# Sliding-window attention scores as three products of split operands instead of one full-precision product

## What is computed

```python
q = split_heads(hidden_states @ wq)      # 16 heads of 128
k = split_heads(hidden_states @ wk)
v = split_heads(hidden_states @ wv)
q = _apply_rotary(q, cos, sin)
k = _apply_rotary(k, cos, sin)
valid = (k_pos > q_pos - WINDOW) & (k_pos <= q_pos)      # WINDOW is 256, Ln is 256
attn = jnp.einsum('bhqd,bhkd->bhqk', q, k) * scale
attn = jnp.where(valid, attn, neg)
attn = jax.nn.softmax(attn, axis=-1)
out = jnp.einsum('bhqk,bhkd->bhqd', attn, v)
return out @ wo
```

## Time and profile before

| | |
|---|---|
| time, median of 3 runs | 2634.21 us (2633.89 to 2636.63) |
| the profiled execution | 2631.4 us, of which the span of its instructions is 2629.7 us |
| self-attention (units 0 to 31) | about 36 to 1890 us of the span |
| context attention | about 1890 to 2280 us |
| experts | the rest |
| PE busy | 2512.0 us, 96% of the span |
| DVE, ACT, POOL busy | 1875.7, 958.9, 861.5 us |

### The profile page before, as it was taken

The page is one execution under the profiler, slowest core; times in us unless marked ns, Lnnn a source line. Parts: engine busy times, 40 slices in busy tenths (PEclk is TensorE's granted clock), DMA queues, the critical chain, the costliest instruction groups (busy, mean ns, idle before and its releaser), DMA issues. The chain is left out here.

```text
span 2629.7 us, 36626 instructions
## 1 busy us (share of the span) xinstructions
PE 2512.0 (96%) x12424; PEld 1885.8 (72%) x12424; DVE 1875.7 (71%) x3978; ACT 958.9 (36%) x2434; POOL 861.5 (33%) x696
## 2 busy tenths in 40 slices
PE   6999999999999999999999999999889999998894
PEld 5788888888888888888888888888634444442673
DVE  5887887666667666666766677777768878885657
ACT  2323223322222232222233222223257777776220
POOL 3211112321111232111123211122258888887000
PEclk8999999999999999999999999999989999999897
DMA  3222233221222222122222212222356676661003
GB/s 120 65 81 94 102 120 125 90 81 65 84 100 73 86 91 81 65 91 96 71 88 89 81 64 81 99 78 89 117 177 218 221 226 221 215 213 60 21 1 128
DMA packets 170150, 280.56 MB, mean 107 GB/s; under 512 B 15088, under 2 KB 81648, under 8 KB 169968
## 3 DMA queue, kind: packets, MB, share of 16 engines
q1 hardware_dynamic: 169968, 278.23, 31.4%
HBM read 185.37 MB, written 92.27 MB: 106 GB/s over the span
## 5 line engine op out<-in xcount | busy, mean ns | idle before, releaser
L539 PE MATMUL pj<-xnt,whi 128*128 128x512 f32 x2048 | 718.9, 412 | 7.3 <-DVE xnt L926 7.3
L705 ACT ACTIVATE pr<-sc,nmx 128x128 f32<-128x128 f32 (+1 forms) x512 | 210.6, 416 | 1011.2 <-DVE nmx L871 1008.1
L433 POOL TENSOR_TENSOR qt<-rot,swp 128x512 f32<-128x512 f32 x128 | 165.8, 1296 | 1038.0 <-DVE swp L847 1035.3
L539 PEld LDWEIGHTS pj<-xnt,whi 128*128 128x128 f32 x2048 | 388.1, 189 | 87.7 <-DVE xnt L926 8.1
L539 PE MATMUL pj<-xnt,wlo 128*128 128x512 f32 x1024 | 400.7, 391 | 0.0
L536 PE MATMUL pj<-whi,xnt 128*128 128x512 f32 x1024 | 358.5, 411 | 4.1 <-issue 4.1
L459 POOL TENSOR_TENSOR xprt<-xprt,xprt 128x512 f32<-128x512 f32 x256 | 320.6, 1284 | 83.6 <-PE ob L626 83.6
L762 ACT ACTIVATE xprt<-pj 128x512 f32<-128x512 f32 x512 | 290.8, 595 | 145.5 <-PE pj L615 143.9
L845 DVE TENSOR_TENSOR rot<-pj,trig 128x512 f32<-128x512 f32 x256 | 176.4, 689 | 137.2 <-PE pj L539 136.4
L955 DVE TENSOR_REDUCE xnmx<-sc 128x1 f32<-128x512 f32 x342 | 227.2, 680 | 65.0 <-PE sc L604 64.7
L433 POOL TENSOR_TENSOR kt<-rot,swp 128x512 f32<-128x512 f32 x128 | 164.8, 1287 | 304.4 <-DVE swp L847 304.4
(11 more groups left out here) (180 smaller groups left out, 4272.5 us busy)
## 6 DMA issues: line engine op xcount, KB each, us to landing
xnt<-xt_scratch SPq DMA_DIRECT2D x48, 1024.0 KB, 7.1
x_scratch<-xio SPq DMA_DIRECT2D x64, 512.0 KB, 3.6
xio<-x_scratch SPq DMA_DIRECT2D x48, 512.0 KB, 3.9
qst<-sq_scratch SPq DMA_DIRECT2D x192, 128.0 KB, 2.5
kst<-sk_scratch SPq DMA_DIRECT2D x192, 128.0 KB, 2.6
raw<-in_w_all_dram SPq DMA_DIRECT2D x64, 256.0 KB, 4.8
xt_scratch<-xnt SPq DMA_DIRECT2D x16, 1024.0 KB, 8.4
sq_scratch<-qp SPq DMA_DIRECT2D x32, 512.0 KB, 3.4
```

The lines of the kernel that those rows point to most:

```text
L433: nc.gpsimd.tensor_tensor(qk["QK".index(kind)][h][:, :, :].rearrange("p b n -> p (b n)"), rot[r % 2][:, :], swp[r % 2][:, :], ALU.add).the ...
L539: last = nc.tensor.matmul(bank[:, :], wpart[:, w, i * HD:(i + 1) * HD], moving, start=(k == 0), stop=(k == 3 * CB - 1))
L705: nc.scalar.activation(pr[:, a % 4, lo:hi], SC[a % 2][:, lo:hi], ACT.Exp, bias=nmx[:, a % 4, t:t + 1], accum_out=rsum[:, a % 4, t:t + 1]). ...
```

## The change

The turned queries and keys are no longer kept in float32. GpSimd adds in place into `rot`; ScalarE then rounds the sum into `qhi`/`khi` (`turn_round`, new), and GpSimd subtracts to get the rest `qlo`/`klo` (`turn_rest`, new). The scores wait for the rest, and each of the two score tiles is three float32r matmuls. `rope_mul` may reuse a `rot` buffer only after the rest is taken.

The rest parts need 16 KB, which come from the second set of Q weight chunks (and the wlo places beside it). So there is one set; the next group's Q chunks can only be converted after the last Q block of the old group (slot 8), and the weight schedule moves: V in slots 4 to 7, Q and K in slots 9 to 12. The load of the projections' input moves from slot 10 to 14, and the preparation of the context attention in the last unit moves some slots later, with its buffers at other places. The core of the diff:

```diff
-        qk = [[at_x2(f"{n}t{h}", [P, 2, L], F32, 40 + 8 * k + 2 * h) for h in range(HG)] for k, n in enumerate("qk")]
+        qkhi = [[at_x2(f"{n}hi{h}", [P, 2, L], F32R, 40 + 8 * k + 2 * h) for h in range(HG)] for k, n in enumerate("qk")]
+        qklo = [[at(f"{n}lo{h}", [P, 2, L], F32R, 60.5 + 2 * NCH + 40 * k + 2 * h) for h in range(HG)] for k, n in enumerate("qk")]
...
-            return NCH * g + 4 * ("QVKO" if g else "QKVO").index(kind) + c
+            return NCH * g + 4 * ("VQKO" if g else "QKVO").index(kind) + c
...
+        QK_PARTS = [(kind, c) for kind in "QK" for c in range(CB)]
+        QK_AT = ((0, 1, 2), (3, 4), (5, 6), (7,))
...
             if f % PAIRS == PAIRS - 1 and 0 < g < G:
-                if k < 4:
-                    return [(g, "Q", k)]
-                if k < 8:
+                if 4 <= k < 8:
                     return [(g, "V", k - 4)]
-                if k in (10, 11):
-                    return [(g, "K", 2 * (k - 10) + i) for i in range(2)]
+                if 9 <= k < 13:
+                    return [(g, *QK_PARTS[i]) for i in QK_AT[k - 9]]
...
-                if k == 10 and PAIRS <= u + 2 < UNITS:
+                if k == 14 and PAIRS <= u + 2 < UNITS:
                     sp.wait_ge(s_blk, number["K", u, 3] + 1)
                     load_xn(u + 2)
...
             def turn_add(kind, u, h):
                 r = place[kind, u, h]
                 pool.wait_ge(s_mul, r + 1)
-                if u:
-                    pool.wait_ge(s_sc, 8 * (u - 1) + 2 * h + 2)
-                nc.gpsimd.tensor_tensor(qk["QK".index(kind)][h][:, :, :].rearrange("p b n -> p (b n)"), rot[r % 2][:, :],
-                                        swp[r % 2][:, :], ALU.add).then_inc(s_rot, 1)
+                nc.gpsimd.tensor_tensor(rot[r % 2][:, :], rot[r % 2][:, :], swp[r % 2][:, :], ALU.add).then_inc(s_rot, 1)
+
+            def turn_rest(kind, u, h):
+                r, k = place[kind, u, h], "QK".index(kind)
+                pool.wait_ge(s_qkhi, r + 1)
+                nc.gpsimd.tensor_tensor(qklo[k][h][:, :, :].rearrange("p b n -> p (b n)"), rot[r % 2][:, :],
+                                        qkhi[k][h][:, :, :].rearrange("p b n -> p (b n)").bitcast(F32),
+                                        ALU.subtract).then_inc(s_qklo, 1)
...
             for s in range(-3, LAST + 1):
+                if s - 2 in at and at[s - 2][0] in "QK":
+                    turn_rest(*at[s - 2])
                 if s - 1 in at and at[s - 1][0] in "QK":
                     turn_add(*at[s - 1])
...
             def scores(a):
                 u, h, b = a // 8, a % 8 // 2, a % 2
-                pe.wait_ge(s_rot, place["K", u, h] + 1)
+                pe.wait_ge(s_qklo, place["K", u, h] + 1)
                 if a >= 2:
                     pe.wait_ge(s_exp, 2 * a - 2)
-                bank, qT, kT = SC[a % 2], qk[0][h][:, b, :], qk[1][h][:, b, :]
-                nc.tensor.matmul(bank[:, 0:P], qT[:, 0:P], kT[:, 0:P], start=True, stop=True)
-                nc.tensor.matmul(bank[:, P:3 * P], qT[:, P:2 * P], kT[:, 0:2 * P], start=True,
-                                 stop=True).then_inc(s_sc, 1)
+                bank, (qhi, khi), (qlo, klo) = SC[a % 2], (part[h][:, b, :] for part in qkhi), (part[h][:, b, :] for part in qklo)
+                for t in range(TB):
+                    out, rows, cols = bank[:, t * P:(2 * t + 1) * P], slice(t * P, (t + 1) * P), slice(0, (t + 1) * P)
+                    for k, (q, x) in enumerate(((qhi, khi), (qhi, klo), (qlo, khi))):
+                        last = nc.tensor.matmul(out, q[:, rows], x[:, cols], start=(k == 0), stop=(k == 2))
+                last.then_inc(s_sc, 1)
...
+            def turn_round(kind, u, h):
+                r = place[kind, u, h]
+                act.wait_ge(s_rot, r + 1)
+                if u:
+                    act.wait_ge(s_sc, 8 * (u - 1) + 2 * h + 2)
+                nc.scalar.activation(qkhi["QK".index(kind)][h][:, :, :].rearrange("p b n -> p (b n)"), rot[r % 2][:, :],
+                                     ACT.Copy).then_inc(s_qkhi, 1)
...
                 if s - 1 in at and at[s - 1][0] == "V":
                     v_evac(*at[s - 1][1:])
+                if s - 2 in at and at[s - 2][0] in "QK":
+                    turn_round(*at[s - 2])
...
                 if r >= 2:
-                    dve.wait_ge(s_rot, r - 1)
+                    dve.wait_ge(s_qklo, r - 1)
```

More of the change, by code:

```diff
@@ L109, in attention_stages @@
         mlo = at("xmlo", [XPT * CB, P], F32R, 27)
-        STACK_AT = (CH_V, NCH, CH_K)
+        STACK_AT = (CH_Q, CH_K, NCH)
         qst = [at(f"qst{i}", [P, XPT, D], F32R, 60.5 + 2 * STACK_AT[i]) for i in range(STACKS)]
         kst = [at(f"kst{i}", [P, XPT, D], F32R, 100.5 + 2 * STACK_AT[i]) for i in range(STACKS)]
-        qp = [at(f"qp{i}", [P, 2, D], F32R, 60.5 + 4 * i) for i in range(2)]
-        kp = [at(f"kp{i}", [P, 2, D], F32R, 100.5 + 4 * i) for i in range(2)]
+        qp = [at(f"qp{i}", [P, 2, D], F32R, 60.5 + 2 * CH_V + 4 * i) for i in range(2)]
+        kp = [at(f"kp{i}", [P, 2, D], F32R, 100.5 + 2 * CH_V + 4 * i) for i in range(2)]
         RING_AT = (60.5 + 2 * CH_O, 100.5 + 2 * CH_O, 28.5, 36.5, 44.5, 52.5)
@@ L134, in attention_stages @@
         s_mul, s_rot = sem("a_mul"), sem("a_rot")
+        s_qkhi, s_qklo = sem("a_qkhi"), sem("a_qklo")
         s_vev = sem("a_vev")
@@ L202, in chunk_of @@
         def chunk_of(g, kind, c):
[L204 to L206 removed]
+            return {"Q": CH_Q, "K": CH_K, "V": CH_V, "O": CH_O}[kind] + c
+        QK_PARTS = [(kind, c) for kind in "QK" for c in range(CB)]
+        QK_AT = ((0, 1, 2), (3, 4), (5, 6), (7,))
         def converted(s):
@@ L319, in read_stacks @@
                 sp.wait_ge(c_kw[m % 2], 16 * (m // 2) + 16)
-                if m < STACKS:
-                    sp.wait_ge(s_blk, number["VQK"[m], LASTU, 3] + 1)
+                if m < 2:
+                    sp.wait_ge(s_blk, number["QK"[m], LASTU, 3] + 1)
+                if m == 2:
+                    sp.wait_ge(s_sc, STEPS)
                 if m >= STACKS:
@@ L376, in _ @@
                     load_values(1)
-                if s == TAIL:
+                if s == TAIL + 6:
                     write_queries(0)
                     write_keys(0)
-                if s == TAIL + 3:
+                if s == TAIL + 8:
                     write_queries(1)
@@ L383, in _ @@
                     load_context(3)
-                if s == TAIL + 5:
+                if s == TAIL + 9:
                     read_stacks(0)
-                if s == TAIL + 6:
+                if s == TAIL + 11:
+                    read_stacks(1)
                     write_queries(2)
                     write_keys(2)
-                if s == TAIL + 10:
-                    read_stacks(1)
                 if s == TAIL + MAX_AT + 3:
@@ L478, in _ @@
                     w_rest(*part)
-                if s in (TAIL - 1, TAIL + 2, TAIL + 5):
-                    q_rest((s - TAIL + 1) // 3)
-                    k_rest((s - TAIL + 1) // 3)
-                if s == TAIL + 8:
-                    q_rest(3)
+                if s in (TAIL + 5, TAIL + 7, TAIL + 9):
+                    q_rest((s - TAIL - 5) // 2)
+                    k_rest((s - TAIL - 5) // 2)
+                if s == TAIL + 11:
                     nc.gpsimd.memset(xones[:, :], 1.0).then_inc(c_ones, 1)
                     pool.wait_ge(c_ones, 1)
-                    pool.wait_ge(s_blk, number["V", LASTU, 3] + 1)
+                    pool.wait_ge(s_qklo, 2 * HG * UNITS)
+                    pool.wait_ge(s_blk, number["K", LASTU, 3] + 1)
                     row_of_ones(0)
-                if s == TAIL + 11:
-                    pool.wait_ge(s_rot, 2 * HG * UNITS)
-                    pool.wait_ge(s_blk, number["K", LASTU, 3] + 1)
                     row_of_ones(1)
+                if s == TAIL + 13:
+                    q_rest(3)
+                if s == TAIL + 16:
+                    pool.wait_ge(c_qlo, 4)
+                    pool.wait_ge(s_sc, STEPS)
                     row_of_ones(2)
@@ L807, in _ @@
                     w_round(*part)
-                if s in (TAIL - 2, TAIL + 1, TAIL + 4):
-                    if s == TAIL - 2:
-                        act.wait_ge(s_blk, number["K", LASTU - 1, 3] + 1)
-                    x_normed((s - TAIL + 2) // 3)
-                    q_round((s - TAIL + 2) // 3)
-                    k_round((s - TAIL + 2) // 3)
-                if s == TAIL + 7:
+                if s in (TAIL + 4, TAIL + 6, TAIL + 8):
+                    if s == TAIL + 4:
+                        act.wait_ge(s_blk, number["V", LASTU, 3] + 1)
+                    x_normed((s - TAIL - 4) // 2)
+                    q_round((s - TAIL - 4) // 2)
+                    k_round((s - TAIL - 4) // 2)
+                if s == TAIL + 12:
                     x_normed(3)
```

5 lines of the change are left out of this document (removed).

## The result

| | before | after |
|---|---|---|
| median | 2634.05 us (4 runs) | 2685.37 us (4 runs, 2681.95 to 2693.72) |
| ratio | | 1.0195, 95% interval 1.0181 to 1.021 |
| the profiled execution, and its span | 2631.4, 2629.7 us | 2693.7, 2692.0 us |
| mean granted clock of TensorE | 0.980 | 0.971 |

The change makes the kernel 1.95% slower, 51 us in the medians. The forecast was 1.3% (2669 us, range 2638 to 2715). The profiled execution is the slowest of its four, so the two profiles are 62 us apart; part of that lies in the stretch behind the last score step (751.6 us before, 760.7 after), which varies from 751 to 761 us over the profiles of this series, also between kernels that are the same there. I therefore account for the 53 us that lie ahead of that point.

A forecast was written before the change was run, and what follows sets the result against it. Until the context attention, time was taken as the sum of what PE issues. Terms 11 + 8 + 1 + 10.5 + 4 = 34.5 us on 2631.4 gave 2666, with 2.8 for the median 2669 us; range 2638 to 2715.

The forecast's parts named there:

- Score step: On PE, six short float32r matmuls take 0.69 to 0.70 us, 0.045 more a step: +11 us in 256 steps.
- rival of hidden loads: Score matmuls run at the 512-column rate, the step costs 0.52 us: 2624 us, faster; chance 0.11.
- slow short matmuls: Score matmuls of 128 columns cost 0.22 us like full-precision ones, step 1.02 us, +95: 2752 us; chance 0.10.
- Way of the keys: In plain units, the rest through ACT and POOL is ready 0.9 us early, so hidden: 0 us.
- second rival: Way of the keys not hidden: POOL or DVE late at three places of 26 plain units, 31 us, 2700; chance 0.13.
- Start: Units 0 and 1: PE waits longer for V's last chunk (+3.9) and for K2 and K3 (+4.5): +8 us.
- Change of groups, first part: Units 7, 15, 23: old stalls of 7.7 us go, late POOL work costs 8.4: +1 us.
- my 8.4 us: Units 7, 15, 23: K3's rest some 1.3 us late and the last K chunk 1.5, 2.8 x 3.
- Second part: End of units 8, 16, 24: POOL's work after the late O1 chunk stalls PE 3.9, 3.3 and 3.3 us: +10.5.
- Clock: Three new waits may each bring a slower PE clock, as after unit 23's wait: +4 us with the one that goes.
- Last unit: Preparation comes later but the read-back still comes before slot 15: 0 us, within -3 and +4.
- rival of stalls that do not come: Moved loads help and the group changes do not stall: +11 us, 2645 us; chance 0.09.

The follow-up runs named there:

- e1: Kernel before with six float32r score matmuls a step, rests left out: 2647.08 us against 2636.1, ratio 1.0043.
- e5: Kernel before with only the load of the projections' input moved from slot 10 to 14: 2625.04 us against 2635.29, ratio 0.9967.
- e3: Changed kernel's weight schedule, single Q set and moved loads, with the old way of the keys and float32 scores: 2631.82 us, 0.9987 of the kernel before.
- e12: e7 with POOL's rests of Q, K and V weight chunks of groups 1 to 3 cut from 512 columns to 8: 2655.00 us, ratio 1.0086.
- e7: Changed kernel with all four O weight chunks asked for at slot 12: 2673.68 us, ratio 1.015, 12 us less than the change.
- e4: Changed kernel with two float32 score matmuls of the rounded parts in place of six, rests still made and waited for: 2675.29 us, ratio 1.0145.
- e8: Changed kernel with the next group's Q and K weight chunks spread 1, 2, 2, 3 over slots 9 to 12: 2689.15 us, one execution.
- e2: Kernel before with six score matmuls and the whole new way of the keys, old weight schedule kept: 2677.44 us, ratio 1.0155.

## Why the prediction was right or wrong

The direction, the likeliest case and the range held. 16 us of 51 are missing from the forecast by the medians, and 19 of 53 by the trace. By its own steps:

- **Score step, +11: right.** Measured +0.034 us by the step and 8.7 in sum. (e1's +11 by the medians has some 5 us of its longer old stalls in it.) Four of the six starts are 0.11 and 0.12 apart as forecast, the loads throughout; the rival of hidden loads (step of 0.52) is false, as is that of slow short matmuls. That the load of 128 columns is the floor fits all rows, but no run has short matmuls that share a load, so it is not shown against another limit of 0.11 us per matmul. The 81 ns that the Trainium skill gives in "TensorE: Matmul & The Clock Gate", section "Back-to-back issue gap", are not reached: 110 here. Nor does the rule of four passes for a float32 product, in the page "FP8 and Floating Point Precision" of the Trainium skill, section "TensorE Precision Notes", give the time of such short ones: the three float32r products took 1.05 times what the float32 product did.
- **Way of the keys, 0: right.** No PE wait in any plain unit; 57.5 us against the 57.6 named. K2's rest ends at 1106.71 in a plain unit and its scores start at 1107.70: 1.0 us early, against the 0.9 counted. The second rival is false. DVE's normalisation, its argument, did get slower beside twice as many instructions of POOL, but only from 1.04 us to 1.12 a step (602 and 515 ns for its two instructions).
- **Start, +8: 10.4.** The first V block waits 5.16 us, 1.0 more and not 3.9. But PE waits 2.9 us more for each of K2 and K3, not 2.25. POOL's rest of K2 starts 1.69 us after its sum, since ACT comes to the rounding only behind exponentials and a copy of the transposed input, and of the slow clock that follows (0.57 from 71.4 to 78.2 us) I had counted nothing. All waits of the start together grow by 7.1 us; about 3 of the 10.4 are clock.
- **Change of groups, first part, +1: the step that failed.** Measured 12.7. The old waits for `olo` do go, as in e5 and e3, but the new stalls are not 8.4 us in sum but 20: K3's rest is 2.67 us late and not 1.3; K2's is 1.13 late, because a V chunk stands before it, in slots that I had not followed; and the clock takes 2.1 to 3.4 us a unit, where I had put it down for units 8, 16 and 24 alone. The cause that I named, eight chunks and two rests on POOL, is the right one (e12). The size failed in the words "followed in order", which gave a result without its count: POOL's nine instructions from Q3's sum on take 11.3 us, and PE comes 8.7 us after their start, which is 2.7 and not 1.3, about one instruction more than I had. The last K chunk, half of my 8.4 us, brings no wait of its own; it shows only in e3.
- **Second part, +10.5: right,** 11.9, with the wait of 4.16 us against the 3.9 forecast in unit 8, for the reason given (e7). That units 16 and 24 wait 4.97 and 2.82 us against 3.3 each evens out, which is luck in part.
- **Clock, +4: 6.2** for these three.
- **Last unit, 0: 3.4,** at the edge of its range. PE waits 1.7 us for a `klo` there, which is new, and 1.3 for `olo`, where it waited 1.6 before; and 3.4 us at half the clock follow. In e4, e8 and e12 the wait is the same and the slow clock is not there: 48.3 to 48.4 us in place of 49.9. e3, with the moved preparation alone, has neither (46.3 us, as before), and e2, with the new way of the keys alone, 47.2. I did not test it further.

The rival of stalls that do not come is false too: they come, and bigger.

## What to carry to other kernels

Replacing a full-precision matmul by three products brought nothing here: at 128 and 256 columns each of the three costs 0.11 to 0.12 us, the spacing of the weight loads, and six of them cost a little more than two float32 ones did. Whether it pays for longer matmuls no run here tried. The price then is in what prepares the operands: an engine that is busy a third of the time has no room at the few places where all its work stands together, so count its instructions there, in order, against the slots that they must fit in. And try the parts of a change alone: the one line that moved a load (e5) was worth 7 to 9 us, while the change as a whole cost 51.
